# Macaron block on one core: joint attention steps on TensorE, and another order of runs

## What is computed

```
x = x + 0.5 * FFN(layernorm(x))
x = x + ATT(layernorm(x))
x = x + 0.5 * FFN(layernorm(x))     # the same weights as the first
FFN(x): expert = argmax of 8 gate logits;  wo @ relu(wi x + b + loraB[expert] loraA[expert] x) + b2      # width 1024
ATT(x): h = rmsnorm(x) * w1;  q, k, v = h wq, h wk, h wv;  16 heads of 16;  i = exp(clip(h wi + bi)), f = sigmoid(h wf + bf)
        C_t = f C_{t-1} + i v k^T,  n_t = f n_{t-1} + i k,  y_t = C_t q / max(|n_t q|, 1)
        x = x + y wo;  x + (silu(g wgate) * (g wup)) wdown,  g = rmsnorm(x) * w2                          # width 704
```

## Time and profile before

| | |
|---|---|
| three runs | 937.07, 939.15, 939.82 us (median 939.15) |
| the profiled execution | 939.06 us, of which the span is 936.9 |
| TensorE busy | 865.0 us (92%), 12744 matmuls |
| VectorE, ScalarE, GpSimd busy | 627.0, 359.0, 244.5 us |
| mean granted clock of TensorE | 0.98 |

### The profile page before, as it was taken

The page is one execution under the profiler, slowest core; times in us unless marked ns, Lnnn a source line. Parts: engine busy times, 40 slices in busy tenths (PEclk is TensorE's granted clock), DMA queues, the critical chain, the costliest instruction groups (busy, mean ns, idle before and its releaser), DMA issues. The chain is left out here.

```text
span 936.9 us, 30800 instructions
## 1 busy us (share of the span) xinstructions
PE 865.0 (92%) x12744; PEld 823.7 (88%) x12744; DVE 627.0 (67%) x1502; ACT 359.0 (38%) x716; POOL 244.5 (26%) x234
## 2 busy tenths in 40 slices
PE   2958889999899998999899999999989989898998
PEld 2947869999799998999899998999979979898998
DVE  5445677585866858486676758677576787687642
ACT  4453152433533344243523436234343452233431
POOL 2013332320422313322322313332042234411110
PEclk9988999999999999999999999999999999999999
DMA  9105434212243202442133312431035035500000
GB/s 263 57 14 140 131 95 126 66 40 70 83 132 86 58 19 55 124 126 58 36 94 116 87 40 73 139 112 35 24 103 154 11 110 140 152 25 2 1 24 23
DMA packets 66313, 76.04 MB, mean 81 GB/s; under 512 B 12702, under 2 KB 48670, under 8 KB 66176
## 3 DMA queue, kind: packets, MB, share of 16 engines
q1 hardware_dynamic: 66176, 74.09, 28.2%
HBM read 56.75 MB, written 17.30 MB: 79 GB/s over the span
## 5 line engine op out<-in xcount | busy, mean ns | idle before, releaser
L644 ACT ACTIVATE r_h<-bank 128x512 fp32r<-128x512 f32 x128 | 76.5, 598 | 233.6 <-PE bank L1128 164.9
L1093 PE MATMUL bank<-xT_hi,wi_hi 128*128 128x256 f32 x512 | 148.1, 289 | 2.6 <-DVE r_l L836 1.8
L1093 PE MATMUL bank<-wo_hi,r_h 128*128 128x256 f32 x512 | 147.7, 288 | 1.1 <-DVE r_l L836 0.5
L1095 PE MATMUL bank<-xT_lo,wi_hi 128*128 128x256 f32 x512 | 144.1, 282 | 0.0
L1094 PE MATMUL bank<-xT_hi,wi_lo 128*128 128x256 f32 x512 | 144.1, 281 | 0.0
L1095 PE MATMUL bank<-wo_lo,r_h 128*128 128x256 f32 x512 | 143.7, 281 | 0.0
L1094 PE MATMUL bank<-wo_hi,r_l 128*128 128x256 f32 x512 | 143.7, 281 | 0.0
L836 DVE SCALAR_TENSOR_TENSOR r_l<-bank,r_h 128x512 fp32r<-128x512 f32 x128 | 87.9, 687 | 82.7 <-ACT r_h L644 82.1
L1093 PE MATMUL bank<-xT_hi,wgu_hi 128*128 128x256 f32 x352 | 103.1, 293 | 0.6 <-DVE gm L845 0.5
L1093 PEld LDWEIGHTS bank<-xT_hi,wi_hi 128*128 128x128 f32 x512 | 97.3, 190 | 5.0 <-DVE r_l L836 2.4
L1093 PEld LDWEIGHTS bank<-wo_hi,r_h 128*128 128x128 f32 x512 | 96.4, 188 | 3.9 <-issue 2.5
(11 more groups left out here) (157 smaller groups left out, 2143.9 us busy)
## 6 DMA issues: line engine op xcount, KB each, us to landing
dm<-f_scratch SPq DMA_DIRECT2D x128, 128.0 KB, 3.0
arena<-parts_scratch SPq DMA_DIRECT2D x96, 128.0 KB
arena<-parts_scratch SPq DMA_DIRECT2D x96, 64.0 KB
arena<-parts_scratch SPq DMA_DIRECT2D x32, 192.0 KB
x<-in_x SPq DMA_DIRECT2D x16, 256.0 KB, 3.0
parts_scratch<-pa SPq DMA_DIRECT2D x64, 64.0 KB
parts_scratch<-pb SPq DMA_DIRECT2D x64, 64.0 KB
parts_scratch<-pc SPq DMA_DIRECT2D x64, 64.0 KB
```

The costliest lines, as they stand in the source:

```text
L644: nc.scalar.activation(flat(r_h[:, n]), U[use % 2][:], ACT.Relu).then_inc(f_rh, 1)
L1093: nc.tensor.matmul(dst, lh, rh, start=first, stop=False, **more)
L1095: return nc.tensor.matmul(dst, lh, rl, start=False, stop=last, **more)
```

## The change

- RUNS begins with 1 of block 0, 1 of block 1, A of block 0, 1 of block 2, A of block 1; the rest is as it was.
- S is one step for both units of a chunk.
- M has a step of its own only for the state's addition of a block's first chunk; every other M step does the addition of the next chunk's state (not at the block's last chunk), both mixes and the carry of its own chunk. Y has two steps left. The state's addition goes to free columns of bank M instead of bank W.
- VectorE's updates of `c_at` are a letter C of their own, and wait for the carry of the chunk before (`a_c`), except at a block's first chunk.
- The strings of ORDER are redrawn for all engines. SyncE's now begins `H X 7A K F 3A 2E K` where it had `H 7A F X F E C E A E A 4K`.

Of the order strings only the beginning of TensorE's is shown.

```diff
-RUNS = [("1", 0), ("A", 0), ("1", 1), ("A", 1), ("1", 2)]
+RUNS = [("1", 0), ("1", 1), ("A", 0), ("1", 2), ("A", 1)]
...
     "PE": """
-        3G U G 5U V 2U V 2U 2V 4U V U V U 2V 2G 5U G U G 2U G U G 7U V 2U V 2U 2V 4U S U V S Y V 2U M 2V M 2S M 2Y M G 2S Y G 3U M 2U M U M Y S U S G 2Y M U G
-        M U G 2U G M Y M 4U Y 2U Y V 2U V M 2U 2V Y U Y 3U V 2U G 2V S G V 4U V 2U V Y U V U G U S M U G U V U G V U G V S 2M S 3U V 2U V 3U 2V 2U Y 2U V 3U V
...
+        3G U G 7U 2V G V U G U V U V 3U G 2U V G V U V 5U 3V 4U V G U V 2U G U V 2U 2V 5U G U G U G U G 9U V 2U G S 2V 2U M V U S M 3U G V Y U Y 2V U M V U S
+        U Y 2U Y 2U M U S U 2Y M Y U Y 2U G U G 3U V S 2U V U V G U M S U G 2U V G 2U V G V M 3U V 4U V U V U G Y V G 2U V 4U V U 2V G 2U Y 3U M G S U G U G Y
+        U S Y 2U M 3U Y M Y 2U V U V 3U Y U V Y V 2U V S 2U V G 2U G 2V 4U V U M S U V U V U M G 2U G Y V 2U S G V U G V M 4U 2V 3U Y U G V U V 2U G U V 3U V
...
@@ -1024,14 +1023,17 @@
                     v.tensor_tensor(pt[:, n % 2], S[n % 2][:], dm[:, n % DMBUFS], ALU.mult).then_inc(a_P, 1)
                     yield
 
-            def Y_():
+            def C_():
+
+                added = M[:, H * HV:H * HV + DC * 4 * HV].rearrange("p (c e m d) -> p c e m d", c=DC, e=2, m=2)
                 for b, j in chunks:
                     n = b * TILES + j
-
-                    added = W[:, 0:DC * 4 * HV].rearrange("p (c e m d) -> p c e m d", c=DC, e=2, m=2)
                     two = lambda t: t.rearrange("p (e d) -> p e d", e=2)
                     end = lambda c, m: cumE[:, c, j * P + m * TH + TH - 1:j * P + m * TH + TH]
                     dve.wait_ge(a_state, n + 1)
+                    if j:
+
+                        dve.wait_ge(a_c, n)
                     dve.wait_ge(a_ex[1], n)
                     if not opens(b, j):
                         dve.wait_ge(d_ce, 16 * DC * (b + 1))
@@ -1052,6 +1054,10 @@
                             v.scalar_tensor_tensor(two(c_at[0][:, c]), two(c_at[1][:, c]), end(c, 1), added[:, c, :, 1],
                                                    ALU.mult, ALU.add).then_inc(a_at[0], 1)
                         yield
+
+            def Y_():
+                for b, j in chunks:
+                    n = b * TILES + j
 
                     heads = M[:, 0:H * HV].rearrange("p (h m d) -> p h m d", m=2, d=HV)
                     sums = heads[:, :, :, HD]
@@ -1083,7 +1089,7 @@
                     v.bn_stats(z_st[:, j], z[:, j]).then_inc(a_zs, 1)
                     yield
 
-            merge("DVE", {"H": H_(), "R": R_(), "G": G_(), "D": D_(), "P": P_(), "Y": Y_()})
+            merge("DVE", {"H": H_(), "R": R_(), "G": G_(), "D": D_(), "P": P_(), "C": C_(), "Y": Y_()})
 
 
         @block.tensor
@@ -1275,11 +1281,10 @@
 
 
             def S_():
-                for b in range(BLOCKS):
-                    for u in range(UNITS):
-                        j, g = divmod(u, NG)
-                        n = UNITS * b + u
-                        pe.wait_ge(d_stack[j % 2], 16 * STACK_LOADS * (2 * b + j // 2 + 1))
+                for b, j in chunks:
+                    pe.wait_ge(d_stack[j % 2], 16 * STACK_LOADS * (2 * b + j // 2 + 1))
+                    for g in range(NG):
+                        n = UNITS * b + NG * j + g
                         if n > 1:
                             pe.wait_ge(a_P, n - 1)
                         for i in range(GH):
@@ -1290,65 +1295,73 @@
                                 done = nc.tensor.matmul(S[n % 2][tile, i * TH:(i + 1) * TH], ks[:, j % 2, h, tile], qs[:, j % 2, h, own],
                                                         start=True, stop=True)
                         done.then_inc(a_S, 1)
-                        yield
+                    yield
 
             def M_():
...
+                def state(b, j):
+
+                    pe.wait_ge(a_wv, NG * (TILES * b + j + 1))
+                    for c in range(DC):
+                        for q in range(COLS):
+                            tile = slice(q * P // COLS, (q + 1) * P // COLS)
+                            of = c * P + q * P // COLS
+                            done = nc.tensor.matmul(M[tile, H * HV + c * 4 * HV:H * HV + (c + 1) * 4 * HV], k32[:, b % 2, j, of:of + P // COLS],
+                                                    wv[:, HH * c + 2 * q:HH * c + 2 * q + 2].rearrange("p h m d -> p (h m d)"),
+                                                    start=True, stop=True)
+                    done.then_inc(a_state, 1)
+
+                heads = M[:, 0:H * HV].rearrange("p (h m d) -> p h m d", m=2, d=HV)
+                for b, j in chunks:
+                    n = TILES * b + j
+                    if j == 0:
+
+                        if n:
+                            pe.wait_ge(a_y, n)
+                            pe.wait_ge(a_at[1], DC * n)
+                            pe.wait_ge(a_at[0], DC * n_on(*chunks[n - 1]))
+                        state(b, j)
+                        yield
+
+                    pe.wait_ge(a_at[1], DC * (n + 1))
+                    pe.wait_ge(a_at[0], DC * n_on(b, j))
+                    if n:
+                        pe.wait_ge(a_y, n)
+                    if j < TILES - 1:
+                        state(b, j + 1)
+                    pe.wait_ge(f_read, a_use(b, A_V + j // 2) + 1)
+
+                    for g in range(NG):
+                        u = NG * n + g
+                        pe.wait_ge(a_P, u + 1)
                         for i in range(GH // 2):
                             pair = GH // 2 * g + i
                             for q in range(COLS):
                                 tile = slice(q * P // COLS, (q + 1) * P // COLS)
                                 of = (2 * i + q // 2) * TH + q % 2 * (P // COLS)
...
+                                done = nc.tensor.matmul(M[tile, pair * 2 * HV:(pair + 1) * 2 * HV], pt[:, u % 2, of:of + P // COLS],
                                                         values(b, j)[:, 2 * pair + q // 2].rearrange("p m d -> p (m d)"),
                                                         start=pair == 0, stop=False, skip_group_check=True)
                         done.then_inc(a_O, 1)
-                        yield
...
-                        yield
+                    pe.wait_ge(a_ex[1], n + 1)
+                    pe.wait_ge(a_qc, DC * (b + 1))
+                    if not opens(b, j):
+                        pe.wait_ge(a_ex[0], n_on(*chunks[n - 1]))
+                    for m in range(1 if opens(b, j) else 0, 2):
+                        for c in range(DC):
+                            for q in range(COLS):
+                                tile = slice(q * P // COLS, (q + 1) * P // COLS)
+                                t = j * P + m * TH + q % 2 * (P // COLS)
+                                of = c_ex[m][:, c].rearrange("p (h e d) -> p h e d", e=2, d=HV)[:, :, q // 2]
+                                done = nc.tensor.matmul(heads[tile, HH // 2 * c:HH // 2 * (c + 1), m], q32[:, b % 2, c, t:t + P // COLS], of,
+                                                        start=False, stop=True, skip_group_check=True)
+                    done.then_inc(a_c, 1)
+                    yield
 
             def Y_():
                 for b, j in chunks:
                     n = b * TILES + j
                     if n:
                         pe.wait_ge(a_zz, n)
...
                     pe.wait_ge(a_y, n + 1)
                     for c in range(DC):
                         done = nc.tensor.transpose(W[:, c * P:(c + 1) * P], y[:, c * P:(c + 1) * P], ident[:])
```

More of the change, by code:

```diff
@@ L98 @@
[L98 to L101, removed]
@@ L129 @@
+        Y A G A G W 2Q W Y 2W 2Y G Y W G W Y G W Y G W G 2Y 3A 2G W Q W A Q Y 3W G 2Y W Y 2G Y W G W G 2Y 3A G Y Q W A G 2W Y W Q G W Y W 2Y 2G 2W Y G Y 2A Y
+        A 2G Q G A W Q G 3W Y W Y G Y W 2A Y W Y W A 2Y W G W A Y W Q Y W Q G 2Y W G 2W 2Y W 2Y 6G""",
     "SP": """
[L130 to L131 removed]
@@ L1310, in M_ @@
                                 of = (2 * i + q // 2) * TH + q % 2 * (P // COLS)
-                                done = nc.tensor.matmul(M[tile, pair * 2 * HV:(pair + 1) * 2 * HV], pt[:, n % 2, of:of + P // COLS],
+                                done = nc.tensor.matmul(M[tile, pair * 2 * HV:(pair + 1) * 2 * HV], pt[:, u % 2, of:of + P // COLS],
                                                         values(b, j)[:, 2 * pair + q // 2].rearrange("p m d -> p (m d)"),
@@ L1314, in M_ @@
                         done.then_inc(a_O, 1)
-                        yield
-                        if g < NG - 1:
-                            continue
-                        c_n = TILES * b + j
-                        pe.wait_ge(a_ex[1], c_n + 1)
-                        pe.wait_ge(a_qc, DC * (b + 1))
-                        if not opens(b, j):
-                            pe.wait_ge(a_ex[0], n_on(*chunks[c_n - 1]))
-                        heads = M[:, 0:H * HV].rearrange("p (h m d) -> p h m d", m=2, d=HV)
```

(24 more changed lines are left out.)

67 lines of the change are left out of this document (30 added, 37 removed).

## The result

The changed kernel takes 946.09 us (median of 12, 941.54 to 950.46), the kernel before, run beside it, 935.96 (12, 931.63 to 941.54). The ratio is 1.0107, 95% interval 1.008 to 1.0135: slower by 1.1%, where 924 us was forecast. The profiled execution of after took 941.54 us; against before's 939.06 it shows only 2.5 us of the difference, for it is the fastest of its twelve, while before's lies 3.1 us above the median of before.

The account below looks back on a forecast made before the run. TensorE, busy 865.0 of 936.9 us, was taken as the bound; -8.9 - 12.6 - 4.5 + 2 + 4 + 4 + 1 = -15.0 from 939.15 us gave 924 us, range 906 to 944.

Parts of the forecast that it names:

- Joint steps: TensorE's order: 42 fewer groups of 32-column matmuls between 128-column products, 0.30 us each, -12.6 us.
- The order of runs: Start of block 0's attention: block 1's first FFN put before it closes TensorE's stop and low clock, -8.9 us.
- Waits that shrink: TensorE's waits for `z`, for attention's transposes, and for `y` and `yT_lo` get shorter, half counted: -4.5 us.
- What it adds: Four new waits on TensorE from the new order and shared bank: +2, +4, +4 and +1 us.
- The state at the head of M(j): Joint M step begins with the next chunk's state, so everything behind it waits for `wv`: +2 us (0 to +49).
- The routing: Last routing transposes wait for VectorE's choice, with little work left to cover it at four places: +4 us (0 to +8).
- The hole at block 0 and L0's door: L of block 0 follows A1's last projections directly, nothing between its first transposes and products: +4 us (0 to +8).
- The shared bank M: State and mixes share a bank, so carry update and carry step of neighbouring chunks wait for each other: +1 us.
- 947 us: Slower rival: ring loads stand behind score-operand loads on SyncE, so M waits for `wv` over 10 us in total; chance 0.15.
- Round trips: Rival: VectorE round trips set the A stretches, so fewer groups and earlier transposes gain nothing there; 935 us, chance 0.19.

Follow-up runs that it names:

- experiment 3: Tiny matmuls ahead of the first transposes, shifting TensorE's program by half or whole packets; in the changed kernel, half a packet made it 9.3 us faster.
- experiment 4: The kernel before with 21 triples of M and 10 pairs of S drawn together in TensorE's order, all else untouched: 955.43 us, ratio 1.0192.
- old list, small -> joint: Old list of passes, orders drawn by one search: joint steps against small steps (947.38 us), +3.3 us.
- new list, small -> joint: New list of passes, orders drawn by one search: joint steps (959.4 us) against small steps (930.7 us), +28.7 us.
- half-packet kernel: The changed kernel with 32 tiny matmuls (128 instructions, half a packet) ahead of the first transposes: 936.78 us.
- experiment 1: Old or new list of passes times small or joint steps, four kernels with searched orders; control with old list and small steps 947.38 us.
- 945.47: New list, joint steps, searched order (959.4 us), with 36 tiny matmuls (144 instructions) ahead of the first transposes: 945.47 us.
- 930.71: New list of passes with the old small steps, searched order, no tiny matmuls: 930.71 us, 16.7 us under the old list with small steps.
- new-joint: The changed program, new list and joint steps, with its order drawn by the search: 959.4 us.
- new-small: New list of passes with the old small steps, order drawn by the same search: 930.71 us.
- old-joint: Old list of passes with joint steps, order drawn by the same search: +3.3 us against the old list with small steps.
- old-small: The program of before, old list and small steps, with its order drawn anew by the search: 947.38 us.

## Why the prediction was wrong

**The failed step is "Joint steps", -12.6 us.** It failed twice over. First, it left out what a denser stream asks of the instruction supply. "No matmul is added or removed" is true; but 256 instructions of 32-column matmuls, some 10 ns each, run in under 3.4 us if nothing stands between, and then TensorE waits for its own program. The small steps of before, laced with 128-column products at 0.12 us, spread them. Missing term: +10.0 us in the profile (5.9 to 15.9), 9 to 10 us by experiment 3.

Second, the gain itself did not reach the time, and this is the larger part of the miss: with the packets moved, after takes 936.78 us and not 924. The 42 groups fewer are there (114 to 72). Counted over the start times of the traces, the way in and out of a group is 0.25 us on average in before (0.30 at the place of the earlier trace rows), and less of it is spent after. But the steps between equal shapes became slower by nearly as much. All in us, waits counted from 0.15 us on:

```
                                 groups      time outside waits   at changes   other 128-   other 32-    waits,        other
                                                                  of shape     col. steps   col. steps   "issue"       waits
before -> after                  114 -> 72    869.8 -> 866.6       -11.2        +4.8         +3.2        6.1 -> 16.8   61.0 -> 56.0
before -> experiment 4           114 -> 86    869.8 -> 870.1        -7.1        +3.2         +4.1        6.1 -> 18.7   61.0 -> 64.8
old list, small -> joint         108 -> 66    869.1 -> 868.5        -8.5        +2.5         +5.4        9.1 -> 10.6   66.0 -> 69.3
new list, small -> joint         113 -> 64    867.0 -> 867.6        -9.3        +3.4         +6.4        2.0 -> 21.1   60.2 -> 68.9
```

In the three pairs that differ in the steps and not in the list, TensorE's time outside waits is the same within 0.6 us. One part of what is given back is the clock: the mean granted clock is lower in each joint kernel (0.973 against 0.980; 0.977 against 0.980; 0.964 against 0.977; 0.970 against 0.978). Whether the rest is the supply of instructions again, in stops under 0.15 us, is not shown. For the two profiled executions the account closes. Forecast were -14.5 us outside waits (-12.6, and 1.9 of low clock in "The order of runs") and -0.5 of waits; seen are -3.2 outside waits, +10.7 of "issue" and -5.0 of other waits, together the +2.5. The medians differ by 7.6 us more, which no profile shows.

**The order of runs, -8.9**, was right in place and size: 40 to 80 us hold 39.4 us of TensorE's work instead of 25.3, at full clock. The routing laced into A0's projections stops as before, now at 80 to 100 us (6.7 us idle, clock 0.73); over 40 to 100 us TensorE works 8.2 us more. The half-packet kernel reaches L0's first product at 167.0 us, 8.2 ahead of before's 175.2; after itself at 175.0: of these 8.0 us 4.8 lie in three stops in block 0's attention. For the new list speaks its kernel with small steps, against it the pair with joint steps of experiment 1.

**Waits that shrink, -4.5**, came out near its size, but not where I had put it. `z` went (2.9), and so did the waits of later transposes for `xn` (3.0); the first one of all rose from 9.2 to 10.4. The 3.0 us expected from `y` and `yT_lo` did not come: 7.9 us in both kernels. That y's transposes wait 2.7 us longer for `y` may come from the joint M step, which puts its carry last and so leaves less work behind it; no run separates this. Score operands are now waited for, 4.7 us, which stood in no term.

**What it adds.** The state at the head of M(j): TensorE waited 1.1 us for `wv` (+2 taken). The routing: +3.9 on `u_rep` (+4 taken), right. The hole at block 0 and L0's door: 160 to 180 us holds 14.04 us of work, 6.0 lost where 4 was taken, but 2.09 us of it is a packet's stop. The shared bank M: no wait for it is among the listed ones.

**The rivals.** 947 us was on the table with 0.15, and the time came out there; its mechanism did not (needed: over 10 us on `wv`; seen: 1.1). "Round trips" asked for TensorE as busy around each A as before, and that sign came: 15.69 against 16.19 in 240 to 260, and after has no stop of "issue" in this stretch, where before has one of 0.8 us; it waits for `u_rep` 1.9 us, `gm` 1.7 and `xT_lo` 0.7. From the first to the last projection of A, over blocks 2 to 7, waits other than "issue" rose from 14.4 to 18.2 us. Its 935 us and the 10.0 us of stops that no case had would make 945; but this rival still had 5.7 us from groups elsewhere, and the table above shows 3.2 at most. No run separates the round trips from the rest. The range ended at 944 and did not hold the 946.

**Open.** Joint and small steps with the new list differ by 28.7 us; the packets explain 17.5 by their stops, or 13.9 by the shift; the kernels of 945.47 and 930.71 still differ by 14.8 with 5.3 us of stops between them. And a packet sometimes begins late: TensorE passed from one packet into the next at 157.28 us, and the transfer of the one after began at 161.49, 4.2 us later, where about 0.9 us is the median over the 20 traces. Much data was moving then (0.45 of the DMA engines' time in 160 to 180 us), but that isn't needed for it: in the kernel of experiment 4 TensorE passed into a packet at 345.44 us, and the next began 3.94 us later though nothing else moved. The DMA view of 344 to 350 us:

```profile
DMA packets 1, 0.02 MB, mean 3 GB/s; under 512 B 0, under 2 KB 0, under 8 KB 0
```

The longest stop of that kernel (3.22 us at 805.93) also follows a packet that began 3.3 us after TensorE had passed into the one before. What makes them late stays open.

## What to carry to other kernels

Where a stream of very short instructions is made denser, look for stops marked "issue" on the engine and count at which instruction they stand; if the number repeats modulo 256, the engine waits for its program, and the cure is to keep long instructions between the short ones, not to join them. Before believing a difference of 1% between two versions of such a kernel, shift the whole program by half a packet and time it again: here this alone was worth 9 to 10 us. Price a term that removes steps together with what the removed gaps had covered, and look in one trace whether the time outside waits falls by it: here it did not.

## What the runs showed of the hardware

- TensorE's program is fetched during the run in packets of 16 KB, 256 instructions of 64 bytes (102 packets here). The Trainium skill says in its overview only that the instruction streams are moved to each engine when the program is loaded ("Trainium Architecture — The Big Picture", The software stack); the trace shows the packets spread over the whole span, so here the measurement decides.
- It stops where a packet ends if 256 instructions ran in less than about 3.4 us; it goes on 2.5 us (2.15 to 3.09) after the packet's transfer has begun. In the middle case a packet begins about 0.9 us after TensorE passes into the one before it, which with the 2.5 makes the 3.4. The 3.4 is fitted, and the sum depends on which instruction is taken as the first of a packet: summed over the start times it gives 7.5, 14.5, 16.9, 0.4, 10.9 and 5.7 us for before, after, and the new-joint, new-small, old-joint and old-small kernels; seen were 5.9, 15.9, 19.1, 1.6, 10.6 and 7.2.
- An isolated tiny fp32 matmul in TensorE's full stream costs 0.19 us, with a change of shape 0.30.
